# Softmax maxima of cross attention: from TensorE's matmuls to a VectorE transpose and DMAs

## The reference

```python
kv_rope = kv_c * cos[None] + _rotate_half(kv_c) * sin[None]
q_r = jnp.einsum('bshq,hqr->bhsr', q_big, W_qr)      # q_big from layernorm(x) @ Wq.T, per head
k_r = jnp.einsum('bld,hdr->bhlr', kv_rope, W_kr)
scores = jnp.einsum('bhsr,bhlr->bhsl', q_r, k_r)
attn = jax.nn.softmax(scores, axis=-1)               # subtracts the maximum of each row
ctx_c = jnp.einsum('bhsl,bld->bhsd', attn, kv_rope)
out = jnp.einsum('bhsd,hkd->bshk', ctx_c, w_kc_kv).reshape(b, s, H * K) @ Wo.T
x = x + out                                          # then the feed-forward block over x
```

## Time and profile before

| What | Value |
|---|---|
| Median of 3 runs | 1196.5 us (1196.28 to 1198.25) |
| The profiled execution | 1192.87 us, its span 1191.1 us |
| Busy, share of the span | PE 93%, POOL 75%, DVE 74%, ACT 56% |
| Chain that ended last | PE 85%, DVE 7%, issue 3%, DMA 2% |
| Mean granted TensorE clock | 0.961 |

### The profile page before, as it was taken

The page is one execution under the profiler, slowest core; times in us unless marked ns, Lnnn a source line. Parts: engine busy times, 40 slices in busy tenths (PEclk is TensorE's granted clock), DMA queues, the critical chain, the costliest instruction groups (busy, mean ns, idle before and its releaser), DMA issues.

```text
span 1191.1 us, 39790 instructions
## 1 busy us (share of the span) xinstructions
PE 1104.9 (93%) x14852; PEld 735.9 (62%) x14852; DVE 882.1 (74%) x1573; ACT 670.9 (56%) x1195; POOL 889.8 (75%) x956
## 2 busy tenths in 40 slices
PE   5879999999999998999999999999999999999361
PEld 4636666666666665666666666666676666667240
DVE  4377778777787777777878687777877787887448
ACT  1445566566665665565656665566656565567322
POOL 0329887898788976798788877897879877787713
PEclk9989999999999999999999999999999999999655
DMA  9020001000100001000100001000100020000002
GB/s 331 40 78 14 14 14 27 14 16 15 30 16 14 12 14 33 14 14 12 30 16 16 15 16 29 12 15 16 29 13 13 14 86 16 15 15 3 1 2 71
DMA packets 41288, 34.69 MB, mean 29 GB/s; under 512 B 7608, under 2 KB 38648, under 8 KB 40640
## 3 DMA queue, kind: packets, MB, share of 16 engines
q1 hardware_dynamic: 40512, 27.79, 8.3%
q10 hardware_dynamic: 576, 4.19, 1.0%
HBM read 17.27 MB, written 2.10 MB: 16 GB/s over the span
## 4 chain that ended last, share of the span: by engine, by line
PE 85%; DVE 7%; issue 3%; DMA 2%; ACT 1%; POOL 1%; SPq 1%; DVEq 0%; ACTq 0%; POOLq 0%
PE ps_s L740 14%; PE ps_s L739 14%; PE ps_m L610 13%; PE ps_o L658 8%; PE ps_o L661 8%; PE ps_o L668 8%; PE ps_x L598 3%; PE ps_x L684 3%; PE ps_x L621 2%; DVE mx L934 1%; PE ps_x L545 1%; PE ps_x L676 1%; PE ps_x L544 1%; DMA plo_all<-wqr_dram 1%; PE ps_x L711 1%
## 5 line engine op out<-in xcount | busy, mean ns | idle before, releaser
L207 POOL TENSOR_TENSOR plo_all<-big 128x512 f16<-128x512 f32 x640 | 683.3, 1085 | 213.8 <-ACT big L459 213.0
L934 DVE TENSOR_REDUCE mx<-ps_m 128x1 f32<-128x512 f32 (+1 forms) x832 | 544.7, 666 | 218.6 <-PE ps_m L610 188.2
L459 ACT ACTIVATE big<-ps_s 128x512 f32<-128x512 f32 x768 | 458.4, 598 | 342.2 <-PE ps_s L740 341.1
L739 PE MATMUL ps_s<-qq,k_hi 128*128 128x512 f16 (+1 forms) x832 | 316.2, 380 | 5.6 <-issue 5.6
L740 PE MATMUL ps_s<-qq,k_lo 96*128 96x512 f16 (+1 forms) x832 | 318.0, 382 | 0.0
L610 PE MATMUL ps_m<-k_hi,qq 128*128 128x512 f16 x768 | 293.1, 382 | 5.1 <-ACT k_lo L378 2.3
L658 PEld LDWEIGHTS ps_o<-k,big 128*128 128x128 bf16 x3072 | 184.9, 98 | 119.8 <-issue 1.1
L661 PE MATMUL ps_o<-k,big 128*128 128x64 f16 x3072 | 219.8, 193 | 0.0
L668 PE MATMUL ps_o<-k,plo_all 128*128 128x65 f16 x3072 | 218.2, 193 | 0.0
L658 PE MATMUL ps_o<-k,big 128*128 128x65 f16 x3072 | 218.1, 193 | 0.0
L207 DVE TENSOR_TENSOR plo_all<-big 128x512 f16<-128x512 f32 x128 | 172.3, 1346 | 0.0
(11 more groups left out here) (200 smaller groups left out, 998.4 us busy)
## 6 DMA issues: line engine op xcount, KB each, us to landing
qq<-q_hi SPq DMA_DIRECT2D x256, 32.0 KB, 1.9
qq<-q_lo SPq DMA_DIRECT2D x128, 32.0 KB, 1.9
tables<-kv_dram SPq DMA_DIRECT2D x8, 384.0 KB
big<-wq_dram ACTq DMA_DIRECT2D x1, 2048.0 KB, 15.5
xs<-x_dram SPq DMA_DIRECT2D x4, 512.0 KB, 18.0
big<-wo_t_dram SPq DMA_DIRECT2D x1, 2048.0 KB, 13.1
tables<-d_w_dram SPq DMA_DIRECT2D x2, 1024.0 KB, 6.9
out_dram<-big SPq DMA_DIRECT2D x8, 256.0 KB, 2.2
```

Of the source, the lines that this page charges most:

```text
L207: eng.tensor_tensor(probs_lo(t)[0:r, :], probs(t)[0:r, :], probs_hi(t)[0:r, :], ALU.subtract).then_inc(done, 1)
L459: act.activation(probs(t)[0:r, :], ps_s[0:r, (p * KT + t) % 2, :], ACT.Exp, scale=1.0 / SC).then_inc(p_done, 1)
L739: pe.matmul(ps_s[0:r, j % 2, :], k_hi[par][:, c], qq[p % 4][:, 0, :], start=True, stop=False)
L934: dve.tensor_reduce(o, i, AX.X, ALU.max).then_inc(mx_read, 1)
```

## The change

The four matmuls `max_row`, the ScalarE copy and the bf16 identity go. VectorE now reduces to a float32 negm, scales it by 1/16 into the first 4 of 32 columns of negh (fp16), and transposes negh in blocks of 32 x 32 into negt: rows 32 b to 32 b + 3 of negt then hold, for i = 0 to 3, the maxima of queries 128 i + 32 b to 128 i + 32 b + 31. SyncE moves them with four DMAs (b = 0 to 3), each of 4 rows of 64 bytes, to row 64 of qq. `move_maxima` stands behind `move_queries` in SyncE's order, and in the prologue ahead of 13 loads. TensorE waits for in_max instead of mrow_copied. EARLY becomes 4, while `ctx_low` keeps its step 10.

```diff
-EARLY = 3
+EARLY = 4
...
-        negm = sb("negm", [128, 4], BF16)
+        negm = sb("negm", [128, 4])
+        negh = sb("negh", [128, 32], F16)
+        negt = sb("negt", [128, 32], F16)
...
+            def move_maxima(p, g):
+
+                sp.wait_ge(negt_done, g + 1)
+                row = qq[p % 4][64:65, 1, :].rearrange("o (i b q) -> o b i q", i=4, b=4)
+                for b in range(4):
+                    sp.dma_start(row[:, b, :, :], negt[32 * b:32 * b + 4, :]).then_inc(in_max, 16)
+
             move_queries(0, 0)
             move_queries(1, 1)
+            move_maxima(0, 0)
             sp.dma_start(gw[:, :, :], gate_w.rearrange("(t p) m -> p t m", p=128)).then_inc(in_gate, 16)
...
-                for p in range(NP - 2 if last(n) else NP):
-                    move_queries((p + 2) % NP, n * NP + p + 2)
+                for p in range(NP):
+                    if not (last(n) and p >= NP - 2):
+                        move_queries((p + 2) % NP, n * NP + p + 2)
+                    if not (last(n) and p == NP - 1):
+                        move_maxima((p + 1) % NP, n * NP + p + 1)
...
-            def copy_row(p, g):
-
-                act.wait_ge(mrow_done, g + 1)
-                copy(qq[p % 4][64:65, 1, :], ps_x[64:65, :], scale=1.0 / SC).then_inc(mrow_copied, 1)
...
-            def max_row(g):
-
-                pe.wait_ge(negm_done, g + 1)
-                for i in range(4):
-                    mm = pe.matmul(ps_x[64:65, i * 128:(i + 1) * 128], negm[:, i:i + 1], identb[:, :], start=True, stop=True)
-                mm.then_inc(mrow_done, 1)
...
                         if t == 0:
-                            pe.wait_ge(mrow_copied, g + 1)
+                            pe.wait_ge(in_max, g * 64 + 64)
...
-                        if t == 11 and ahead:
-                            take_x((mrow_copied, g + 2))
-                            max_row(g + 1)
...
             def negate_max(p, g):
 
                 dve.wait_ge(mx_read, g * MX_OPS + MX_OPS)
+                dve.tensor_reduce(negm[:, :], mxs[p % 2][:, :].rearrange("p (k i) -> p i k", k=4), AX.X, ALU.max,
+                                  negate=True).then_inc(negm_done, 1)
+                dve.wait_ge(negm_done, g + 1)
+                dve.tensor_scalar(negh[:, 0:4], negm[:, :], 1.0 / SC, None, ALU.mult).then_inc(negh_done, 1)
                 if not (isinstance(g, int) and g == 0):
-                    dve.wait_ge(mrow_done, g)
-                with nc.allow_low_precision("a shift that cancels in the softmax"):
-                    dve.tensor_reduce(negm[:, :], mxs[p % 2][:, :].rearrange("p (k i) -> p i k", k=4), AX.X, ALU.max,
-                                      negate=True).then_inc(negm_done, 1)
+                    dve.wait_ge(in_max, g * 64)
+                dve.wait_ge(negh_done, g + 1)
+                dve.transpose(negt[:, :], negh[:, :]).then_inc(negt_done, 1)
...
-                        if t == KT - EARLY and started:
+                        if t == 10 and started:
                             ctx_low(par if p else 1 - par, (p - 1) % NP, g - 1)
```

More of the change, by code:

```diff
@@ L93, in build_xattn_ffn @@
         mxs = [sb(f"mx{i}", [128, 16]) for i in range(2)]
-        negm = sb("negm", [128, 4], BF16)
+        negm = sb("negm", [128, 4])
+        negh = sb("negh", [128, 32], F16)
+        negt = sb("negt", [128, 32], F16)
         ident = sb("ident", [128, 128])
-        identb = sb("identb", [128, 128], BF16)
         identh = sb("identh", [128, 128], F16)
@@ L163, in build_xattn_ffn @@
         mx_done, mx_read, negm_done = sem("mx_done"), sem("mx_read"), sem("negm_done")
-        mrow_done, mrow_copied = sem("mrow_done"), sem("mrow_copied")
+        negh_done, negt_done, in_max = sem("negh_done"), sem("negt_done"), sem("in_max")
         st_done, p_done, lo_d, lo_p, pv_done = (sem(s) for s in ("st_done", "p_done", "lo_d", "lo_p", "pv_done"))
@@ L298, in keys @@
                         pool.wait_ge(in_tab, 32)
-                        pool.wait_ge(pads, 15)
+                        pool.wait_ge(pads, 16)
                 else:
@@ L436, in ctx_high @@
                 copy(ctx_n[par][:, p, 0:S], ps_x[:, 0:S]).then_inc(ct_copied, 1)
-            act.wait_ge(pads, 15)
+            act.wait_ge(pads, 16)
             high_part(0, 0)
@@ L446, in _ @@
                      scale=SW).then_inc(fold_copied, 1)
-            copy_row(0, 0)
             def batch(n, par):
@@ L466, in batch @@
                             ctx_high(par if p else 1 - par, (p - 1) % NP, g - 1)
-                        if t == 11 and not (last(n) and p == NP - 1):
-                            copy_row(p + 1, g + 1)
                         if t == 12 and not last(n) and p in (3, 6):
@@ L583, in _ @@
             pe.wait_ge(fold_copied, 6)
-            pe.wait_ge(dve_const, 2)
+            pe.wait_ge(dve_const, 1)
             for i in range(3):
@@ L643, in _ @@
             pe.wait_ge(kt_copied, 4)
-            max_row(0)
             pe.wait_ge(in_qq[1], QQ_DMAS)
@@ L716, in batch @@
                 m = n - 1
-                free = (mrow_copied, n * NP + 1)
+                free = (ql_done, 2) if first(n) else (ct_low, n * NP - 1)
                 def take_x(after):
@@ L868, in _ @@
                 pad(qq[i][64:96, 1, :], 0.0)
+            pad(negh[:, 4:32], 0.0)
             pad(consts[:, 0, :], 1.5)
@@ L871, in _ @@
             dve.wait_ge(in_small, 16)
-            dve.tensor_copy(identb[:, :], ident[:, :]).then_inc(dve_const, 1)
             dve.tensor_copy(identh[:, :], ident[:, :]).then_inc(dve_const, 1)
```

## The result

| | Before | After |
|---|---|---|
| Median | 1196.39 us (1196.02 to 1198.25, 4 runs) | 1220.05 us (1216.03 to 1222.78, 4 runs) |
| Profiled execution, its span | 1192.87, 1191.1 us | 1218.38, 1216.6 us |
| Mean granted TensorE clock | 0.961 | 0.959 |

The ratio is 1.0192 (95% interval 1.0158 to 1.0225). The medians are 23.7 us apart (the ratio makes it 23.0), where 9.1 were forecast. The time lies inside the stated range and the sign was right; the size was not.

The account below looks back on a forecast made before the run. TensorE was taken to bound the kernel. L621 -26.5, step 0 waits +20.0, +3.3 and +2.2, keys +5.6, queries +1.5 and prologue +3.0 made +9.1 us on the 1196.5 median: 1205.6 us, range 1180 to 1242.

Parts of the forecast that it names:

- the sign: Whole kernel: the change was forecast to make it slower, at 60%.
- L621 is worth 0.42 us a pair: Step 11 on TensorE: removing the four row-of-maxima matmuls gives back 0.42 us a pair, 26.5 us over 63.
- The scaling waits for GpSimd: New VectorE scaling of the maxima: it waits until GpSimd's running operation ends, taken as 1.03 us, bounds 0.17 and 1.04.
- the quiet pair: Pair 0 of batch 4, on whose times the new path was worked out: a 0.74 us wait at step 0.
- The transpose, 0.20 us, free of that wait: VectorE's transpose after the scaling: 0.20 us with a 0.03 gap, not sitting out a GpSimd operation.
- +52 us rival: Transpose waiting for GpSimd: 1.04 us at 41 boundaries, about +52 us; listed under the slow rival, 18%.
- An issue costs 0.40: SyncE's four transfers of the row: each takes 0.40 us to issue, with gaps of 0.04; range ends 0.29 and 0.75.
- The 0.75 of L283: Upper bound for a row transfer's issue, from a DMA read as spreading one partition's row: +70.8 us; slow rival, 18%.
- 27 bare boundaries at 0.74, pair 6 at 0.47, pair 4 at 0.31, 5.6 for the keys: Step 0 waits: 20.0 us where no step 12 work covers them, 3.3, 2.2; key loads behind maxima at batch ends, 5.6.
- Queries needed one step earlier, 1.5 us: Step 9: low queries needed one step sooner with 0.2 us of slack, 1.5 us in all, bounds 0 and 63 x 0.2.
- Prologue +3.0: Start: TensorE starts 2.2 us later and pair 2's queries come late, +3.0 us in all, bounds 2.2 and 3.7.

Follow-up runs that it names:

- experiment 1: The kernel before with only its maxima four steps ahead instead of three: 1216.3 us, ratio 1.0171 to the kernel before.
- experiment 3: The changed kernel with EARLY at 3 instead of 4, the rest as changed: 1255.98 us, ratio 1.0496 to the kernel before.
- n2: Changed kernel with three steps ahead, no scaling, late wait, one ordered transfer for the row, high queries copied twice: 1198.47 us, ratio 1.0018 to before.
- experiment 11: The run n2: changed kernel, three steps ahead, no scaling, the row in one ordered transfer: 1198.47 us, ratio 1.0018 to the kernel before.
- experiment 6: The changed kernel with the last two of the row's four transfers issued by ScalarE instead of SyncE: 1200.95 us, ratio 1.0047 to the kernel before.

## Why the prediction was right and wrong

- *L621 is worth 0.42 us a pair*: right, -26.3 in all, step 11 shorter by 0.42 to 0.43 in every pair.
- *The scaling waits for GpSimd*: right. 0.95 us in the example, 1.03 in the sum, 0.588 in the median, and removing it, with its own 0.17 us, gave back 17 to 18 us. Its length goes by the pair: 1.02 us in pairs 0 and 6, 0.94 in 5 and 7, 0.17 to 0.22 in 1 to 3, 0.38 in 4 (means over batches 1 to 6), so the quiet pair stood for fewer boundaries than I gave it. The Trainium skill, "SBUF — State Buffer", section "Who interferes with whom", has tensor_scalar among the operations that can take the port pair shared with GpSimd; the trace agrees (0.170 to 1.036 us for one shape).
- *The transpose, 0.20 us, free of that wait*: right, 0.211 to 0.214 in all 64. The +52 us rival falls.
- *An issue costs 0.40*: wrong, 0.572 and up. (The 0.75 of L283 that bounded it goes the other way, from one partition to several.) Over three issues and their gaps the chain is 1.96 us (597.05 to 599.01) and not 1.32. The landing gave some of it back: 1.60 us behind the last issue's start instead of 1.70. In all a bare boundary with a waiting scaling is late by 1.24 us, not 0.74: 6.47 us lie between step 8 and step 0, in pairs 0 and 6 alike, where 5.63 - 0.42 + 0.03 = 5.24 would without a wait. The total hides it, as the next point shows.
- *27 bare boundaries at 0.74, pair 6 at 0.47, pair 4 at 0.31, 5.6 for the keys*: the sum came out near (27.9 against 31.1) by luck. Pair 6 got 0.96, which is 1.24 less the 0.27 of its keys. Pair 0 got only 0.67 because its late queries had taken the rest in step 9 (1.15 us there and 0.24 at step 0 in batch 3, 0.45 and 0.87 in batch 5: together always about 1.24 above the usual 0.09). Pair 2 got 0.60 with a scaling of 0.22 us, because L617 came 1.12 us late. Pair 4 got 0.10. The keys cost little: pair 7 waits 1.24 to 1.27 in four of seven batches, no more than a boundary without keys, and 1.53 in one; in the other two (0.45 and 0.55) the stretch was already 8.8 and 8.3 us long before the change.
- *Queries needed one step earlier, 1.5 us*: **this is the step that failed.** The steps in question grew by 18.4 us, some 11 of them for late low queries. I worked it out on one quiet pair, where 0.2 us of slack was left, and put a bound of 63 x 0.2 us on it. The late ones are neither rare nor within 0.2: TensorE waits 17 times after and once before (experiment 1), and steps 9 in the loop are up to 1.2 us longer for it. One pair on from the example:

```profile
605.90 3.44 SPq L253 DMA_DIRECT2D qq<-q_hi  x4
609.38 1.25 SPq L256 DMA_DIRECT2D qq<-q_lo  x2
```

```profile
612.03 0.39 PE L614 MATMUL ps_m<-k_hi,qq 128*128 128x512 f16 x1 [0.65 <-DMA qq<-q_lo]
```

  The four q_hi issues took 3.44 us here, against the 2.39 of the earlier trace rows on which the slack rested. The row had said it: 0.461 at the least, 2.074 at the most. I used its median and left out its spread.
- *Not in the forecast at all*: pair 2. VectorE is one read behind there, since the projection's normalisation lies among its reads. The last maxima matmul overwrites the bank that read number 10 (from 0) frees. At three steps ahead it comes one step later and finds the bank free; at four it starts when the read, the first of the three here, ends:

```profile
646.38 0.29 PE L617 MATMUL ps_m<-k_hi,qq 128*128 128x65 f16 x4 [0.96 <-DVE mx L927]
```

```profile
645.64 1.61 DVE L927 TENSOR_REDUCE mx<-ps_m 128x1 f32<-128x512 f32 x3
```

  That is 0.71 us a pair, 5 us in all. I had asked of VectorE only whether its sum of work fits into a pair (it does: a mean), not whether each read comes in time for the bank that L617 overwrites. With three steps this wait falls from 7.5 us to 0.8 (experiment 3); no run changed the order of VectorE's reads.
- *Prologue +3.0*: right in size, 3.5, and in its cause, the queries of pair 2 (step 9 of the first pair is 3.1 us longer). The first L735 starts at 79.98, though, 0.6 us later than before and not 2.2. The new DMAs stand ahead of 17 loads there (15 of weights and 2 of keys), not 13; the sum used their measured time and doesn't change.

With 18.4 in the place of 1.5 and the measured 27.9 in the place of 31.1 the sum is +23. EARLY at 4 was counted with almost no price. It costs 20 us alone (experiment 1), the start included; going back to 3 costs 36 on balance (experiment 3; the trace, of its slowest execution, has 44 of lateness at step 0 and 21 in steps at a lower clock, against 18 won back). The versions that gain, by 12 to 14 us, are those in which the path is short, the queries come in time and the wait stands behind the first matmul of step 0. One of the same kind (n2) gained nothing, for a reason elsewhere.

## What to carry over

Moving work a step earlier moves a deadline for all that feeds it: work out the slack of each feeder at its late instances (minimum, median and maximum of the issue), not in one quiet stretch, and for buffers read instance by instance rather than by an engine's mean load. A wait that is put right may come back at the next one: late queries and a late row shared their time here, and a term that matched in the total had two errors in it. Where small DMAs end a critical path, look at their number before their bytes (4 rows or 16 made no difference here), so find a layout in which one transfer does it, or spread them over two queues. And put a wait directly in front of the instruction that reads what it waits for.

## What the runs showed of the hardware

- A DMA of 4 rows of 64 bytes between two places of SBUF costs SyncE 0.572 us or more to issue; one of 16 rows 0.523 in the median, one of 64 rows 0.461 at the least and 0.597 in the median, up to 2.074 (kernel before). In the example it lands 1.0 us behind the issue's end (1.60 from its start); with two queues, 1.91 and 2.04 from its start were seen.
- Issues on SyncE and ScalarE at one time overlap: 0.638 and 0.588 us in the median, against 0.573 on SyncE alone (experiment 6).
- VectorE's TENSOR_TENSOR with two inputs in SBUF can wait for several operations of GpSimd in a row: 4.23 us in the example, 5.30 at the most (0.68 at the least), beside GpSimd operations of 1.04 (experiment 11):

```profile
L210 DVE TENSOR_TENSOR plo_all<-big x128: 679/1298/5297, 83.8 to 1105.9; 128x512 f16<-128x512 f32 x128
```

  The Trainium skill, "SBUF — State Buffer", section "Who interferes with whom", says that a VectorE instruction with two SBUF inputs contends with a GpSimd instruction that reads SBUF, under an exclusive lock, and that issue order decides who blocks. If whoever was issued first also got the next turn, a waiting operation would lose one; here it sat out two in one version and four in another, and the measurement decides.
- TensorE's granted clock fell after waits of some 2 us that stood between stretches of full work: behind one of 2.23 us it was 1.00 for 1 us, then 0.63, 0.50, 0.50 and 0.66 in the next four (experiment 11); behind one of 2.09 us, 0.60 and 0.50 over 3.6 us (experiment 3). The waits of some 1.1 us at step 0 in the loop of after left no longer steps behind them (the two steps behind the one at 600.83 took 1.18 and 1.02 us, at a clock of 1.00).
